# A one-core attention and mixture-of-experts kernel: two TensorE transposes per batch are replaced by SBUF-to-SBUF transposing DMAs

## The reference, cut to what matters

```python
x = x + xattn(layernorm(x), ctx_768, ...)
def ffn(x, gate_w, w1, w2):                      # x: layernorm of the sum above
    router_logits = einsum('bsd,de->bse', x, gate_w)
    top_logits, top_idx = top_k(router_logits, 2)
    ...
    h = silu(einsum('bsd,edf->ebsf', x, w1))
    y = einsum('ebsf,efd->ebsd', h, w2)
    return einsum('ebsd,bse->bsd', y, combine)
x = x + ffn(layernorm(x), ...)
```

## Time and profile before

| what | us |
|---|---|
| median of 3 runs (714.78 to 716.4) | 716.13 |
| the profiled execution's own time | 715.26 |
| its span in the trace | 713.5 |
| first score product of body 0 / body 1 / body 2 | 67.10 / 93.90 / 119.37 |
| first score product of body 14 / body 15 | 433.76 / 459.96 |
| first product of the expert stage | 494.75 |

### The profile page before, as it was taken

The page is one execution under the profiler, slowest core; times in us unless marked ns, Lnnn a source line. Parts: engine busy times, 40 slices in busy tenths (PEclk is TensorE's granted clock), DMA queues, the critical chain, the costliest instruction groups (busy, mean ns, idle before and its releaser), DMA issues. The chain is left out here.

```text
span 713.5 us, 22010 instructions
## 1 busy us (share of the span) xinstructions
PE 639.0 (90%) x7612; PEld 528.3 (74%) x7613; DVE 519.7 (73%) x1226; ACT 446.3 (63%) x768; POOL 483.3 (68%) x577
## 2 busy tenths in 40 slices
PE   6627799999999999999999999979999999999871
PEld 2215587788788888788788778757888888888751
DVE  3964679988988998898898898986577644445431
ACT  1436787778778778778778877854464454454330
POOL 3024645878878877977877887875677676556744
PEclk9999899999999999999999999999999999999997
DMA  8921111112111121111211211203769989655630
GB/s 263 322 79 21 32 34 52 48 45 68 47 55 57 47 62 50 59 53 48 75 36 48 80 32 48 78 16 77 119 124 136 133 119 139 92 82 87 86 48 6
DMA packets 87259, 55.31 MB, mean 78 GB/s; under 512 B 60784, under 2 KB 81520, under 8 KB 87216
## 3 DMA queue, kind: packets, MB, share of 16 engines
q1 hardware_dynamic: 73840, 37.41, 22.2%
q0 software_dynamic: 13376, 17.33, 13.4%
HBM read 20.27 MB, written 24.85 MB: 63 GB/s over the span
## 5 line engine op out<-in xcount | busy, mean ns | idle before, releaser
L527 POOL DMA_INDIRECT out_x<-pt_s,token_of x71 | 113.0, 1592 | 23.4 <-issue 21.4
L782 DVE TENSOR_TENSOR wq_s<-wk_s,wq_s 128x512 f16<-128x512 f32 (+1 forms) x78 | 51.5, 664 | 78.6 <-ACT wq_s L603 78.5
L598 ACT ACTIVATE wk_s<-ps 128x512 f32<-128x512 f32 (+1 forms) x78 | 43.5, 557 | 102.9 <-PE ps L1600 99.0
L1600 PE MATMUL ps<-ffnw,wq_s 128*128 x852 | 100.1, 273 | 6.3 <-DVE wq_s L782 4.8
L1600 PE MATMUL ps<-q_s,ffnw 128*128 128x256 f16 (+1 forms) x936 | 103.3, 264 | 2.1 <-issue 1.6
L959 POOL TENSOR_TENSOR prob<-prob,mx 128x1168 f32<-128x1168 f32 x64 | 77.6, 1233 | 37.6 <-DVE mx L1401 37.5
L1600 PEld LDWEIGHTS ps<-q_s,ffnw 128*128 x936 | 86.0, 98 | 15.2 <-issue 4.6
L1600 PEld LDWEIGHTS ps<-ffnw,wq_s 128*128 128x128 f16 x852 | 81.7, 98 | 19.8 <-issue 9.8
L1600 PE MATMUL ps<-wo_s,ot_s 128*128 128x256 f16 x768 | 89.4, 273 | 2.8 <-DVE ot_s L1338 2.8
L1600 PE MATMUL ps<-xt_s,wq_s 128*128 128x256 f16 x768 | 89.9, 279 | 1.9 <-DVE xt_s L1338 1.9
L1600 PEld LDWEIGHTS ps<-xt_s,wq_s 128*128 128x128 f16 x768 | 76.5, 100 | 13.0 <-issue 1.9
(11 more groups left out here) (232 smaller groups left out, 1176.0 us busy)
## 6 DMA issues: line engine op xcount, KB each, us to landing
wstage<-in_ffn_w SPq DMA_DIRECT2D x16, 512.0 KB, 3.6
x_sb<-in_x SPq DMA_DIRECT2D x4, 1024.0 KB, 10.8
out_x<-x_sb SPq DMA_DIRECT2D x16, 256.0 KB, 2.2
rows_dram<-wstage SPq DMA_DIRECT2D x8, 264.0 KB
out_x<-pt_s,token_of POOLq DMA_INDIRECT x71
pt_s<-in_wq SPq DMA_DIRECT2D x2, 512.0 KB, 4.4
pt_s<-in_wo SPq DMA_DIRECT2D x2, 512.0 KB, 8.4
rows_dram<-row_words,slot_i POOLq DMA_INDIRECT x64, 2.5
```

Source lines behind the costliest of these rows:

```text
L527: pool.indirect_dma_start(out_rows, bass.IndirectOffsetOnAxis(ap=token_of[:, j % UNROLL, c:c + 1], axis=0), y_sb[:, j % UNROLL, c, :], Non ...
L598: act.activation(h32[:, half, 0:2 * n], h_ps(t, j, half)[:, 0:2 * n], ACT.Silu, scale=1 / WSCALE).then_inc(silu_done, 1)
L782: dve.tensor_tensor(hs[:, j % 2, 1, 2 * half:2 * half + 2, 0:n], h32[:, half, 0:2 * n].rearrange("p (f n) -> p f n", f=2), hs[:, j % 2, 0, ...
L1600: last = pe.matmul(o, lhs(a, n), rhs(c, n), start=(i == 0), stop=(i == len(steps) - 1))
```

## The change

- `normalise_x` writes to PSUM (bank 1). ACT makes the fp16 high part `xh` from there (`x_high`), DVE the low part (`x_low`), and SP turns both with two transposing DMAs from SBUF to SBUF (`columns_x`), two batches ahead. Batches 0 and 1 are still turned by TensorE.
- The second layer norm's rows (high and low part, as they go to the scatter) are turned by two such DMAs (`columns_2`). `transpose_2` and `x2t_copy` go. The router takes three fp16 products for each fp32 one, on a split `gate_w`, and moves to just behind the first scores of the body after.
- `row_words` has two slots, so that bodies are written in pairs; 0 to 3, 14 and 15 stand singly.
- The order changes on ACT (`normalise_2` and `row_high` after the fifth `pt`), DVE (sums of the second half before `residual`), POOL and SP.

```diff
 def ... SP:
+            def columns_x(b):
+                for t in range(TPB):
+                    sp.dma_start_transpose(xt_s[:].rearrange("p a k n -> p (a k) n")[:, :, t * P:t * P + P],
+                                           xh[:, t].rearrange("p a d -> p (a d)")).then_inc(xt_in, 16)
+            def columns_2(slot):
+                for t in range(TPB):
+                    sp.dma_start_transpose(x2t[:, :, t * P:t * P + P], row[:, slot, t, 0:META]).then_inc(x2_in, 16)
+            def body(b, par, first, last, x_left):
                 if not last:
                     sp.wait_ge(k_mm, b + 1)
                     context_rest(ctx_k, b + 1, ctx_k_in)
-                if not first:
-                    store_x1(b - 1)
-                if not last:
                     sp.wait_ge(v_mm, b + 1)
                     context_rest(ctx_v, b + 1, ctx_v_in)
+                if x_left:
+                    columns_x(b + 2)
+                if not first:
+                    sp.wait_ge(row_lo, b + 1)
+                    store_x1(b - 1)
+                    columns_2(1 - par)
+                if not last:
                     sp.wait_ge(fw_split, b + 1)
                     sp.dma_start(wstage[:], ffn_w[...]).then_inc(fw_in, 16)
...
 POOL:
                 shift(b, 1)
                 normalise(b, 0)
-                if routed and not last:
-                    scatter(b - 2, 0)
-                if not first and not last:
-                    rstd_2(b - 1)
                 normalise(b, 1)
...
+                if not first:
+                    rstd_2(b - 1)
+                if routed:
+                    scatter(b - 2, par, 0)
+                if not first:
+                    row_low(b - 1, 1 - par)
                 if routed and not last:
-                    scatter(b - 2, 1)
+                    scatter(b - 2, par, 1)
                 pool.wait_ge(fw_hi, b + 1)
                 pool.tensor_tensor(fw[1], wstage[:], fw[0], ALU.subtract).then_inc(fw_split, 1)
                 if last:
-                    scatter(b - 2, 1)
+                    scatter(b - 2, par, 1)
                 else:
                     add_bias(b)
-                    if not first:
-                        row_low(b - 1)
...
 ACT:
+            def x_high(b):
+                if not (isinstance(b, int) and b < 3):
+                    act.wait_ge(xt_in, 32 * b - 64)
+                act.wait_ge(xn_done, b + 1)
+                act.activation(xh[:, :, 0, :], x_rows(), ACT.Copy).then_inc(xh_hi, 1)
...
                 copy_scores(b, 0)
-                if not last:
-                    xt(b + 1)
+                if first:
+                    xt(1)
...
                 exp(b, 0)
                 if x_left:
-                    normalise_x(b + 2)
+                    act.wait_ge(s_copied, 2 * b + 2)
+                    normalise_x(b + 2, x_rows())
+                    x_high(b + 2)
...
                 pt(b, 1)
-                if not first and not last:
-                    normalise_2(b - 1)
...
                 pt(b, 4)
-                if last:
+                if not first:
                     normalise_2(b - 1)
+                    row_high(b - 1, 1 - par)
                 pt(b, 5)
-                if not first and not last:
-                    x2t_copy(b - 1)
...
                 ot(b, 1)
-                if not first and not last:
-                    row_high(b - 1)
...
 DVE:
                 sums(b, 0)
+                if x_left:
+                    x_low(b + 2)
                 if not last:
                     q(b + 1, 0)
                     q(b + 1, 1)
+                sums(b, 1)
                 if not first:
                     residual(b - 1)
-                sums(b, 1)
...
+                place = rank_bank(b)[:, 4 * EXPERTS:6 * EXPERTS].rearrange("p (t e) -> p t e", t=TPB)
...
 PE:
             def router(b):
-                pe.wait_ge(x2_copied, b + 1)
+                pe.wait_ge(x2_in, 32 * b + 32)
                 for t in range(TPB):
                     c = t * EXPERTS
-                    for kk in range(KD):
-                        last = pe.matmul(router_bank(b)[:, c:c + EXPERTS], x2t[:, kk, t * P:t * P + P], gate_f[:, kk, :],
-                                         start=(kk == 0), stop=(kk == KD - 1))
+                    last = product(router_bank(b)[:, c:c + EXPERTS], lambda a, n: x2t[:, a * KD + n, t * P:t * P + P],
+                                   lambda a, n: gate_h[:, a, n, :], KD)
...
                 scores(b, 0)
-                if not last:
-                    if not first:
-                        pe.wait_ge(ot_split, 4 * b - 3)
-                    transpose_x(b + 1)
+                if first:
+                    transpose_x(1)
+                if not (isinstance(b, int) and b < 2):
+                    if not (isinstance(b, int) and b < 3):
+                        pe.wait_ge(slots, b - 1)
+                    router(b - 2)
                 if not first:
                     project(b - 1, 0)
...
-                    pe.wait_ge(xt_split, b + 2)
+                    if first:
+                        pe.wait_ge(xt_split, 2)
+                    else:
+                        pe.wait_ge(xt_in, 32 * b)
                     queries(b + 1, 0)
...
+                if x_left:
+                    pe.wait_ge(xh_lo, b + 1)
                 new_values(b)
...
-                if not first and not last:
-                    pe.wait_ge(pt_split, 8 * b + 2)
-                    transpose_2(b - 1)
...
-                    if k == 1 and not first and not last:
-                        pe.wait_ge(slots, b)
-                        router(b - 1)
                     attend(b, k)
```

More of the change, by code:

```diff
@@ L893, in _, with last_rows @@
             sp.dma_start(wstage[:], ffn_w[0]).then_inc(fw_in, 16)
[L894 to L898, removed]
+            body(0, 0, True, False, True)
+            body(1, 1, False, False, True)
+            body(2, 0, False, False, True)
+            body(3, 1, False, False, True)
+            with sp.Fori(2, BATCH // 2 - 1) as i:
+                for par in (0, 1):
+                    body(i * 2 + par, par, False, False, True)
+            body(BATCH - 2, 0, False, False, False)
+            body(BATCH - 1, 1, False, True, False)
+            def last_rows():
+                sp.wait_ge(row_lo, BATCH + 1)
+                sp.wait_ge(lg_mm, BATCH - 1)
+                store_x1(BATCH - 1)
+                columns_2(1)
+            ffn_sp(sp, last_rows)
         @block.gpsimd
@@ L1054, in _ @@
             pool.wait_ge(misc_in, 32)
[L1055 to L1058, removed]
+            body(0, 0)
+            body(1, 1)
+            body(2, 0)
+            body(3, 1)
+            with pool.Fori(2, BATCH // 2 - 1) as i:
+                for par in (0, 1):
+                    body(i * 2 + par, par)
+            body(BATCH - 2, 0)
             pool.iota(earlier_half[:], [[16, NH // 2], [0, 2]], base=landed(FULL - 1), channel_multiplier=0,
@@ L1073, in _ @@
                       channel_multiplier=0).then_inc(pad_made, 1)
-            scatter(BATCH - 2, 0)
+            scatter(BATCH - 2, 0, 0)
+            row_low(BATCH - 1, 1)
             def then(t):
@@ L1130, in hi_of, with normalise_x @@
                 act.activation(dst, src, ACT.Copy, scale=scale).then_inc(done, 1)
-            def normalise_x(b):
+            def normalise_x(b, into):
                 for t in range(TPB):
@@ L1192, in normalise_2, with row_high, body @@
                 last.then_inc(x2n_done, 1)
-            def row_high(b):
+            def row_high(b, slot):
                 act.wait_ge(x2n_done, b + 1)
-                act.wait_ge(scattered, 64 * b + 16)
-                act.activation(row[:, :, 0:DM], x2n[:], ACT.Copy).then_inc(row_hi, 1)
-            def x2t_copy(b):
-                act.wait_ge(x2_mm, b + 1)
-                act.activation(x2t[:].rearrange("p k n -> p (k n)"), x2_bank(b), ACT.Copy).then_inc(x2_copied, 1)
+                act.wait_ge(scattered, 16 if isinstance(b, int) and b < 1 else 64 * b - 48)
+                act.activation(row[:, slot, :, 0:DM], x2n[:], ACT.Copy).then_inc(row_hi, 1)
             def gap_e(b):
                 act.wait_ge(gap_done, b + 1)
-                act.activation(gap_exp[:], gap[:], ACT.Exp).then_inc(gap_expd, 1)
-            def body(b, first, last, x_left):
+                act.activation(gap_exp[:], gap[:], ACT.Exp, scale=1 / WSCALE).then_inc(gap_expd, 1)
+            def body(b, par, first, last, x_left):
                 copy_scores(b, 0)
-                if not last:
-                    xt(b + 1)
+                if first:
+                    xt(1)
                 if not (isinstance(b, int) and b < 2):
@@ L1287, in _ @@
             put_kipa(0)
-            normalise_x(1)
-            body(0, True, False, True)
-            body(1, False, False, True)
-            with act.Fori(2, BATCH - 2) as b:
-                body(b, False, False, True)
```

(16 more changed lines are left out.)

154 lines of the change are left out of this document (77 added, 77 removed).

## The result

The changed kernel takes 766.22 us (median of 4 runs, 765.55 to 767.38), the kernel before 716.15 beside it: a ratio of 1.0702, 95% interval 1.0679 to 1.0725. The prediction was 758 us, slower, with a range of 712 to 792. It was right, 8 us too low.

A forecast was written before the change was run, and what follows sets the result against it. TensorE was 90% busy, but a chain through the second exponential was as long, beside a weight-load loop with 1.4 us slack. The terms added 41.8 to 715.26 us: 757.1, carried over to 758; range 712 to 792.

The forecast's parts named there:

- bodies 2 to 14: Main loop: bodies 3 to 14 get 3.0 us longer each, 36 in all; body 2 gets 2.5 longer.
- bodies 0 and 1: First two bodies of the loop: 0.3 us longer.
- body 15 to the first expert product: End of the loop: late load, late rows and a scatter holding the first tile loads, 3 us, between 1 and 5.
- The order behind E: From E on: `normalise_2` and `row_high` delay the last three `pt`; the next body starts at E + 13.7, not 13.37.
- E: End of a body's second exponential, 12.82 us into the body before the change.
- The weight load: `wstage` load, issued later: lands 6.5 us into the body, second copy of scores 3.0 later, next body at 29.2.
- The rows: Second norm's rows, turned by DMA behind `row_low`: land 3.2 us into the next body, where PE wants the router at 0.97.
- The router: On PE behind the first scores: 24 fp16 products in place of 8 fp32, 1.0 us, between 0.7 and 1.2.
- The x path: Transposing DMAs of x, issued over 15 us before use: hidden, as is ACT's wait for them in `x_high`.
- TensorE decides: Rival, from the keys to the last `attend`: TensorE bounds the kernel, body 24.65 us, total 694; chance 9%.
- The waits are covered: Rival: neither load nor rows late, bodies 26.2 to 26.8 us, total 712 to 726, at 719; chance 13%.
- SP is no bound: Denies the rival that four costly transposing issues a body make SP's queue the bound: 870 us at 5 each; chance 12%.

The follow-up runs named there:

- e2: Changed kernel, with GpSimd making the weights' low part right behind `rstd_2` and SP issuing the weight load ahead of its wait for `row_low`: 766.32 us.
- e8: Changed kernel with both edits, the early weight load of e2 and the idle TensorE products of e1: 757.92 us.
- e1: Changed kernel with ten unread products of 512 columns filling TensorE's wait ahead of the router: 755.87 us.
- e5: Kernel before with only x turned by DMA, second norm and router as before: 720.13 us.
- e9: e7 with the weights' low part, then `row_low`, ahead of both scatters, and the weight load issued ahead of the rows' store and turns: 707.49 us.
- e7: Changed kernel, `normalise_2` and `row_high` ahead of the keys, weights' low part ahead of the second scatter, router behind the projection's first half: 722.12 us.

## Why the prediction was right, and where it was off

The profiled execution's span grew by 52.1 us, 713.5 to 765.6; the sum had 41.8. By its own terms:

| term | predicted | measured |
|---|---|---|
| bodies 2 to 14 | 38.5 | 46.7 |
| bodies 0 and 1 | 0.3 | 1.2 |
| body 15 to the first expert product | 3 | 3.6 |
| expert stage | 0 | -0.6 |
| ahead of body 0 | 0 | 1.1 |

*The order behind E.* Predicted 13.7 from E to the next body, measured 13.71 and 13.80. `row_high` at E + 10.55: measured 10.35. POOL waits for it 2.25: 1.86. `row_low` at E + 11.8: 11.58. The weights' low part at E + 16.45: 16.16. All of it could be read from the rows of before and the new program order.

*The weight load.* Predicted to be taken 6.5 into the body, the second copy at 8.76: measured 5.86 and 8.02 in the body at 270.31. ACT takes the load 0.64 earlier than priced, and the body is 28.53 where the clock stays up, not 29.2. POOL frees `wstage` 2.47 into the body, not 2.75, and the load lands 3.2 behind its issue, not 3.6. This term was mis-sized: 2.34 us a body over the 26.19 of before, not 3.0, some 30 us in all.

*The rows.* Taken: one issue of 1.21 and a landing of 3.2, from loads out of DRAM. Measured for the transposing issues from SBUF (source lines of `columns_2`, then `columns_x`; ns min/median/max, landing in us):

```profile
L889 SPq DMA_TRANSPOSE x2t<-row_words x32: 1209/1260/1901, 120.1 to 558.8; - x32
...
DMA to landing us min/median/max: 2.3/3.4/5.0
```

```profile
L883 SPq DMA_TRANSPOSE xt_s<-xh x28: 1257/1295/1968, 88.1 to 470.0; - x28
```

The nearest row was the right one: the router was to start 3.2 into the body and starts at 2.63 to 4.35 in bodies 2 to 14, at 3.43 in the median. That load and rows would hold the body alike was right too (e2, e8). The router was mis-sized: 12 products, 0.33 us until the projection, not 24 and 1.0. With 3.42 and 0.33 the prediction's own sum gives E at 14.8 in place of 15.2; measured 14.76 (body at 270.31).

*What was not priced.* The clock behind PE's wait. The text had a wait of 2 to 3 us ahead of the projection and charged it with its own length; ten of 13 bodies paid 1.3 to 1.7 us more, 16 us in all (e1). The two misses oppose each other, -8 and +16, and leave the 8. The mechanism was right, but that the total came so near is partly luck.

*The x path.* Hidden in the loop, as e5 shows alone. The list of waits of the kernel after has none for the turned x, and one for `x_low`:

```profile
PE ps L1713 <- DVE xh L1406: 3.7, 1, 3.7
```

That one stands in body 0, ahead of the values, and a wait of the values for `x_low` is among the signs that the prediction said would prove it wrong. Body 0 has no projection on PE, so PE gets to the values before `x_low` is done; the cover that the prediction took for every body is missing there. Body 0 is 27.92 us long, before 26.81. This is most of the 1.2 us of bodies 0 and 1 that the sum had at 0.3; how much of it is the wait was not separated.

*The rivals.* "TensorE decides" did not happen in this kernel, but e9 is near its case, with both transfers covered: 25.3 us a body and 707, where the rival had 24.65 and 694. "The waits are covered" did not happen: both load and rows are late. SP is no bound: no issue of a row or an x took over 1.97 us. (That all 39 of the earlier trace rows took 1.2 to 1.3 was misread: eight took over 1.35, the longest 2.11.) The estimate of 13.7 us an issue, worked out from the Trainium skill's page DMA: Bandwidth & Descriptors (section Why a DMA increments its semaphore by 16 and not by 1), does not hold for these transfers: the median is 1.26. Nor do the 1309 ns a block of the Trainium skill's page VectorE: DVE Perf Modes (section The three transpose paths) add up one after the other here: the eight blocks of a batch, 10.5 us that way by estimate, were used 5.8 us after the first issue (297.43 to 303.22).

## What to carry to other kernels

When a step moves to another engine's queue, write down where the moved step stands in that queue and who is behind it. Here a gain of 0.9 us a body was to be had (e9), and four positions (`row_high` behind the keys on ACT, the weights' low part behind `row_low` on POOL, the weight load behind the rows' turns on SP, the router ahead of the projection on PE) turned it into a loss of 3.6. If two waits have one length, remove both before judging either. And a wait on PE is to be priced with the clock of the products behind it.

## What the runs showed of the hardware

*The clock.* PE idle for 1.6 to 3.3 us ahead of the projection was followed by a granted clock of 0.62 to 0.66 over it in some bodies and 1.00 in others. The length of the wait alone does not decide it: 2.38 was followed by 2.78 us of projection, 2.28 by 4.06, and 3.31 by 2.78 (kernel after, bodies at 270.31, 240.42 and 508.99). What else does was not tried.

*VectorE beside GpSimd.* `picked` fell from a median of 1828 ns to 177 when one operand came to lie in PSUM. Before, after, and e7's `picks` with both operands in SBUF (tile views: ns min/median/max):

```profile
L1491 DVE TENSOR_TENSOR picked<-picks,place x16: 180/1828/1841, 124.5 to 516.0; 128x32 f32<-128x32 f16 x16
```

```profile
L1524 DVE TENSOR_TENSOR picked<-picks,ps x16: 175/177/179, 130.8 to 569.5; 128x32 f32<-128x32 f16 x16
```

```profile
L1510 DVE TENSOR_TENSOR picks<-iota,top_i x16: 192/1337/1533, 124.1 to 516.0; 128x32 f16<-128x32 f32 x16
```

In all three kernels GpSimd is inside its 2.43 us of `shift` when these run in the loop (in the kernel after from 306.39, `picked` at 308.42). With both operands in SBUF it ends in the loop within 0.05 us of the end of the GpSimd instruction in which it starts (before, body at 276.60: 283.51, and 283.46 for the first of the two of `shift`); `picks` of the kernel after, which runs outside of `shift`, takes 0.19. The Trainium skill's page SBUF — State Buffer (section SBUF: two separate sides) says that a VectorE operation with two SBUF inputs and a GpSimd operation that reads SBUF share a port pair that is held for the whole instruction; the rows agree, down to 0.18 us for the same operation with an operand in PSUM. On the path it is worth about 0.1 us a body: behind it in DVE's queue stand the second maxima, which start 0.14 us after ACT's copy of the scores in the kernel before (283.76 and 283.62) and 0.03 us in the kernel after (279.60 and 279.57).
